# A product's two weight halves in one transfer instead of two, in a fused attention and gated-FFN layer

## The chip, the cores and the metric

The kernel runs on one core of one Trainium2 chip, as one launch. The time is that of the device in microseconds (us), from the first instruction to the last; lower is better. Before the change it is 2654.52 us, the median of three runs (2654.34 to 2654.75).

## The reference, cut to what matters

```python
x = L0_attn_x                                   # (4, 512, 1024) fp32
xn = _layernorm(x)                              # (x - mean) / sqrt(var + 1e-5)
# attention: 32 query heads, 8 key/value heads, head dimension 128
q, k, v = heads(xn @ Wq.T), heads(xn @ Wk.T), heads(xn @ Wv.T)
q, k = _rmsnorm(q, q_norm_w), _rmsnorm(k, k_norm_w)
scores = einsum('bkgqd,bksd->bkgqs', group(q), k) / sqrt(128)
attn = softmax(scores + causal_alibi_bias)
s = einsum('bkgqs,bksd->bkgqd', attn, v).reshape(b, 512, 4096) @ Wo.T
# gate: a linear layer with 8 low-rank adapters merged into it
g = silu(xn @ W.T + bias + sum_n lora(xn, A[n], B[n]))
return x + s * g
```

## The kernel before, in words

The work is cut into 32 groups n = 8 b + g: b is one of the four sequences, g one of the eight key/value heads. A group is the key head, the value head, four query heads and 128 columns of the gate. Each group has four steps (n, j), one for each query head. Inside a step every engine runs its own list, written out by hand in program order: TensorE (PE) computes scores and the attention product of the head before, turns rows, computes products of the *next* group's projection, then the output projection of an earlier head, then turns this head's probabilities (`step` at L697).

**The projection.** The columns of a group (896 of them, as two halves of 448) are computed by a seven-product scheme over 2 x 2 blocks. The products are called P1, P2, P6, P7, P4, P5, P3 in the order in which they are computed. Group n+1 has P1 and P2 in step (n, 0), P6 and P7 in (n, 1), P4 in (n, 2), P5 and P3 in (n, 3). A product runs for two row tiles t = 0, 1 (`piece`, L538). Its weights are two halves h = 0, 1, each 128 partitions x 896 fp32 values, 448 KB. Every fp32 product is made of three matmuls on a high and a low part of each operand (`three`, L507), so a piece is 12 matmuls: six on half 0, then six on half 1. `w_half` is incremented after half 0 of t = 1, `u_done` after half 1.

**The weights' way.** Halves are numbered w = 14 n + 2 p + h, and half w uses place w % 4 of the buffers `wh` and `wl`. So the two halves of a product lie side by side in places 0, 1 or 2, 3, and a product's places come free when the product two before it is done. SyncE (SP) loads the half from the scratch tensor `wu` in DRAM into `wl` (L302, `load_w`); ScalarE (ACT) copies it into `wh`, rounded (`split_w`, L785 to L788); GpSimd (POOL) subtracts and leaves the low part in `wl` (`low_w`, L1081); then PE may use it (`w_ready`). SP waits for `w_half` before it loads half 0 and for `u_done` before half 1; ACT waits for the half's own semaphore, one of four `w_in`. ACT is told to split P6 and P7 at the end of step (n, 0), P4 and P5 at the end of (n, 1), P3 at the end of (n, 2), P1 and P2 at the end of (n, 3): the first of each pair stands between the first three turned probability tiles and the fourth (`probs_hi`, L858), the second after the fourth. P3 stands there by itself.

**Where the scratch comes from.** In the first sequence the block sums of the weights are still being made. For groups up to 7 SP loads raw weights (`load_weights`, L327), stores three tiles as they are (L347, L348), POOL makes four sums (`weight_sums`, L1132 to L1137), SP stores those (L355), and loads of `wu` wait for these stores (`prep_bst`, `prep_tst`, L299 and L301). All of these are issued by SP in one written order (`step` at L428), so each instruction waits for those ahead of it.

**VectorE (DVE)** works in order as well. At the end of step (n, 2) it makes the low part of the fourth turned tile (L1284), adds the last output bank (L1344), takes two score maxima of the next step (L1319), scales the key rows and the first query rows of group n+1 (L1274), then takes the last two maxima. PE turns those rows (L588) in step (n, 3) before it computes P5.

For the very first P3 the load is issued by ACT (`load_first`, L804 to L812), one half ahead of each of two groups of squares.

Of the kernel before, what the change touches and what calls it, by code (L numbers as in the profile page):

```python
# [7 lines left out]
F32 = mybir.dt.float32  # L8
# [4 lines left out]
H, HKV, HD = 32, 8, 128  # L13
# [9 lines left out]
NG = BATCH * HKV  # L23
# [9 lines left out]
NP = 7  # L33
HW = 2 * NP
P1, P2, P6, P7, P4, P5, P3 = range(NP)
# [8 lines left out]
KEPT = [P1, P2, P3, P5, P7, P4, P6]  # L44
# [25 lines left out]
def loads_into_slot(w):  # L70

    return (w - DIRECT) // 4 + (-1 if w >= LATER else 1)
# [43 lines left out]
def u_count(n, p, t):  # L116
    return HW * n + 2 * p + t + 1
# [10 lines left out]
def build_layer(nc, x_tok, x_first, xT, wa, wo, wT, lora_a, lora_bt, lw, ffn_b, qw, kw, rel, slopes,  # L128
                ident, outT):
    with ExitStack() as ctx:  # L130
        def sb(name, shape, dt=F32):
            return ctx.enter_context(nc.sbuf_tensor(name, shape, dt))
# [4 lines left out]
        def sem(name):  # L137
            return ctx.enter_context(nc.semaphore(name))
# [3 lines left out]
        wu = nc.dram_tensor("wu", [HKV * HW, P, 2 * HALF], F32).ap()  # L142
# [6 lines left out]
        wh, wl = sb("wh", [P, 4, 2, HALF], F32R), sb("wl", [P, 4, 2, HALF], F32R)  # L149
# [38 lines left out]
        weff_out = [sem("weff_out0"), sem("weff_out1")]  # L188
        prep_in, prep_bst = [sem("prep_in0"), sem("prep_in1")], [sem("prep_bst0"), sem("prep_bst1")]
        prep_tst = [sem("prep_tst0"), sem("prep_tst1")]  # L190
        w_in = [sem(f"w_in{i}") for i in range(4)]
        b_in = [sem("b_in0"), sem("b_in1")]
        gate_out = sem("gate_out")
        fin_in = [sem(f"fin_in{i}") for i in range(4)]
# [3 lines left out]
        u_done, w_half = sem("u_done"), sem("w_half")  # L198
# [46 lines left out]
        def prep_tile(g, h, a, c):  # L245

            at = 2 * a + c
            return prep_place(g, h)[:, at * 896:at * 896 + 896].rearrange("p (k n) -> p k n", k=2)
# [21 lines left out]
        def w_slot(t, w, f32=False):  # L270
            ap = t[:, w % 4].rearrange("p k n -> p (k n)")
            return ap.bitcast(F32) if f32 else ap

        def need(eng, semaphore, value):
            if value > 0:
                eng.wait_ge(semaphore, value)
# [6 lines left out]

        @block.sync
        def _(sp):
            def load_w(w):
                if w >= HW * NG:
                    return
                n, at = divmod(w, HW)
                p, h = divmod(at, 2)  # L290
                if w >= 4:
                    n_old, at_old = divmod(w - 4, HW)
                    if h == 0:
                        sp.wait_ge(w_half, NP * n_old + at_old // 2 + 1)
                    else:
                        sp.wait_ge(u_done, u_count(n_old, at_old // 2, 1))
                if n < HKV:
                    if p in (P1, P2, P3):
                        sp.wait_ge(prep_bst[h], 32 * (n + 1))  # L299
                    else:  # L300
                        sp.wait_ge(prep_tst[h], 16 * (n + 1))  # L301
                sp.dma_start(w_slot(wl, w, True), wu[(n % HKV * 2 + h) * NP + KEPT.index(p)]  # L302
                             ).then_inc(w_in[w % 4], 16)

            def load_product(n, p):
                for h in range(2):
                    load_w(HW * n + 2 * p + h)

            def load_b(v):
                if not 0 <= v < NV:  # L310
                    return
                need(sp, out_done, 4 * v - 4)
                if v < 32:
                    sp.wait_ge(wo_copied, 16 * (v + 1))
                sp.dma_start(wb_lo[:, v % 2, :].bitcast(F32), wo_in[v % 32]).then_inc(b_in[v % 2], 16)

            def copy_b(v):
                if v < 32:
                    need(sp, wo_copied, 16 * v)
                    sp.dma_start(wo_in[v], wo[v]).then_inc(wo_copied, 16)  # L320
# [52 lines left out]
            def load_result(b, half):  # L373
                if half == 0 and b + 1 < BATCH:
                    sp.wait_ge(tr_done, TR["x", b + 1, 2 * NP - 1] + 1)
                sp.wait_ge(gate_out, 16 * (HKV * b + 4 * half + 4))
                for c in range(4 * half, 4 * half + 4):
                    x, gate = result_slots(b, c)
                    if b + 1 < BATCH or half == 0:
                        need(sp, res_out[c % 4], 16 * (2 * b + half))  # L380
                    landed = fin_last if b + 1 == BATCH and half == 1 else fin_in
                    sp.dma_start(x, xT[b * NK + c]).then_inc(landed[c % 4], 16)
                    sp.dma_start(gate, gate_dram[b % 2 * NK + c]).then_inc(landed[c % 4], 16)
# [44 lines left out]
            def step(n, j):  # L428
# [23 lines left out]
                if j == 1:  # L452
                    if n == 0:
                        load_product(1, P4)
                    if new is not None:
                        store_halves(new, 0)
                    if n > 0:
                        load_product(n + 1, P4)
                    if g == 0 and ending is not None:
                        store_result(ending, 0)  # L460
                    load_product(n + 1, P5)
# [44 lines left out]
        def _(pe):  # L506
# [59 lines left out]
            def turn_x(key):  # L566
                _, b, f = key
                p = FILLS[f // 2]
                row, col = FILL_AT[p]
                if p in FILL_SUM:  # L570
                    pe.wait_ge(sum_ready, 4 * b + FILL_SUM[p])
                else:
                    if b == 0 and p != P4:
                        pe.wait_ge(x_scaled, 2)
                    else:
                        pe.wait_ge(ln_ready, scaled_rows(b, 4 if p == P4 else 2))
                bank = turn_bank(key)
                for i in range(2):
                    for t in range(2):
                        c = col + (2 * (f % 2) + i) * P  # L580
                        mm = pe.transpose(bank[:, i * 256 + t * P:i * 256 + t * P + P],  # L581
                                          xtok[:, row + t, c:c + P], ident_sb[:])
                mm.then_inc(tr_done, 1)
# [172 lines left out]
        def _(act):  # L756
            act.preload_act_table_set("natural_log_exp_and_others")

            def split_first(p):

                a, c = QUARTER[p]
                for h in range(2):
                    w = 2 * p + h
                    if p in (P1, P2):
                        act.wait_ge(prep_in[h], 128)
                        act.wait_ge(gate_cols, NK)
                    else:
                        act.wait_ge(prep_t[h], 4 if p in (P4, P5) else 3)
                        if h == 0:
                            act.wait_ge(w_half, p - 1)  # L770
                        else:
                            act.wait_ge(u_done, u_count(0, p - 2, 1))
                    act.activation(wh[:, w % 4], prep_tile(0, h, a, c), ACT.Copy).then_inc(w_hi_done, 1)
# [10 lines left out]
            def split_w(w):  # L784
                if w >= HW * NG:  # L785
                    return
                act.wait_ge(w_in[w % 4], 16 * loads_into_slot(w))
                act.activation(w_slot(wh, w), w_slot(wl, w, True), ACT.Copy).then_inc(w_hi_done, 1)  # L788

            def split_later(p, h):  # L790
# [10 lines left out]
                    act.wait_ge(u_done, u_count(0, at // 2, 1))  # L801
                act.activation(wh[:, w % 4], prep_tile(1, h, *QUARTER[p]), ACT.Copy).then_inc(w_hi_done, 1)

            def load_first(h):  # L804

                w = 2 * P3 + h
                if h == 0:
                    act.wait_ge(w_half, P4 + 1)
                else:
                    act.wait_ge(u_done, u_count(0, P4, 1))  # L810
                act.wait_ge(prep_bst[h], 32)
                act.dma_start(w_slot(wl, w, True), wu[h * NP + KEPT.index(P3)]).then_inc(w_in[w % 4], 16)  # L812

            def split_product(n, p):
                for h in range(2):
                    split_w(HW * n + 2 * p + h)
# [21 lines left out]
            def square_rows(n, p, t):  # L838

                if p == P2:  # L840
                    act.wait_ge(u_act, u_act_count(n, P2, t))
                else:
                    act.wait_ge(u_dve, u_dve_count(n, p, t))
                squares(("q0", "q1", "k") if p in (P2, P4) else ("q2", "q3"),
                        t if p in (P2, P3) else t + 2,
                        8 * n + 2 * (P2, P4, P5, P3).index(p) + t)
# [112 lines left out]
            act.wait_ge(fb_in, 16)  # L959
            split_first(P4)  # L960
            split_first(P5)
            for h in range(2):
                load_first(h)
                square_rows(0, P4, h)
            rsqrt(0, 0)
            split_product(0, P3)
# [686 lines left out]
```

## Time and profile before

| what | value |
|---|---|
| median of three runs | 2654.52 us |
| profiled execution, whole | 2655.72 us |
| profiled execution, span | 2653.9 us |
| PE matmul busy | 2583.1 us, 97% |
| PE weight load busy | 2288.9 us, 86% |
| POOL busy | 1718.0 us, 65% |
| ACT busy | 1764.6 us, 66% |
| DVE busy | 1699.8 us, 64% |
| mean granted TensorE clock | 0.995 of full speed |

The profile is one execution. Busy time is time in which an engine has an instruction in work; matmuls overlap one another, so a busy PE is not one without any loss. The page also gives the chain of waits (followed back from the last instruction), the waits of each engine with the instruction that ended them, and for DMA the time from issue to landing. The four waits of interest are: SP for PE (the places come free), ACT for a transfer, POOL for ACT, and PE for POOL or DVE. Line numbers are those of the kernel before.

### The profile page before, as it was taken

To read this page: it belongs to the slowest core of one execution; us is meant where nothing else is said; L and a number is where in the kernel's file an instruction comes from. 1 tells how busy PE (TensorE), PEld (TensorE's weight loads), DVE (VectorE), ACT (ScalarE), POOL (GpSimd) and SP (SyncE) were. 2 spreads that over 40 slices of the span, in tenths; PEclk is the share of its full clock that TensorE was granted. 3 is DMA by queue.
4 is the path that set the end of the run, shared out by engine and by line. 5 is a ranking of instruction groups with operands and counts; after the bars stand their busy time and mean duration, and the time that the engine had idled before them with its cause. 6 is when DMAs were issued, how large, how long until landed. Compare 5 with 4: busy or idle time off the path is not lost.

```text
span 2653.9 us, 39893 instructions
## 1 busy us (share of the span) xinstructions
PE 2583.1 (97%) x13840; PEld 2288.9 (86%) x13840; DVE 1699.8 (64%) x3533; ACT 1764.6 (66%) x4633; POOL 1718.0 (65%) x839
## 2 busy tenths in 40 slices
PE   6789999999999999999999999999999999999997
PEld 5778888888888888888888888888888888888886
DVE  7565656666766665666667666666666756656656
ACT  4565666767767666667766667666777666667764
POOL 3577887785767565655667756565666766656555
PEclk9899999999999999999999999999999999999999
DMA  7868878875354333433344433433334533333323
GB/s 283 289 219 278 265 261 272 271 258 166 118 171 154 113 106 118 140 112 118 106 137 155 128 119 111 144 106 118 109 104 137 189 106 108 115 116 112 112 78 131
DMA packets 171896, 414.78 MB, mean 156 GB/s; under 512 B 31024, under 2 KB 63920, under 8 KB 170800
## 3 DMA queue, kind: packets, MB, share of 16 engines
q1 hardware_dynamic: 170144, 410.19, 47.1%
q8 instruction: 112, 1.84, 0.3%
q10 hardware_dynamic: 1552, 2.04, 0.2%
q14 instruction: 88, 0.72, 0.1%
HBM read 339.81 MB, written 89.13 MB: 162 GB/s over the span
## 4 chain that ended last, share of the span: by engine, by line
PE 90%; DVE 3%; DMA 2%; POOL 2%; ACT 1%; SPq 1%; issue 0%; ACTq 0%; POOLq 0%; DVEq 0%
PE proj L508 21%; PE proj L510 21%; PE proj L509 21%; PE tr L608 5%; PE tr L588 3%; PE sc L508 3%; PE sc L509 3%; PE sc L510 3%; PE ot L509 3%; PE ot L510 3%; PE ot L508 3%; DMA wu<-xtok 1%; PE tr L581 1%; DMA wl<-wu 1%; POOL wl L1081 1%
## 5 line engine op out<-in xcount | busy, mean ns | idle before, releaser
L1081 POOL TENSOR_TENSOR wl<-wl,wh 128x896 fp32r<-128x896 f32 x428 | 909.1, 2156 | 552.3 <-ACT wh L788 552.2
L508 PE MATMUL proj<-wh,xh 128*128 128x448 f32 x1792 | 670.7, 374 | 7.3 <-ACT raw L827 2.2
L509 PE MATMUL proj<-wl,xh 128*128 128x448 f32 x1792 | 657.9, 367 | 0.0
L510 PE MATMUL proj<-wh,xl 128*128 128x448 f32 x1792 | 657.8, 367 | 0.0
L1092 POOL TENSOR_TENSOR wb_lo<-wb_lo,wb_hi 128x1024 fp32r<-128x1024 f32 x128 | 307.7, 2404 | 303.7 <-ACT wb_hi L822 303.7
L879 ACT ACTIVATE misc<-misc,negmax 128x128 f32<-128x128 f32 (+3 forms) x512 | 286.7, 565 | 266.3 <-DVE negmax L1319 266.1
L508 PE MATMUL proj<-o_hi,wb_hi 128*128 128x512 f32 x1024 | 425.2, 415 | 7.4 <-DVE acc L1344 3.5
L1344 DVE TENSOR_TENSOR acc<-acc,proj 128x512 f32<-128x512 f32 x476 | 324.8, 683 | 149.7 <-PE proj L510 147.8
L858 ACT ACTIVATE pT_hi<-tr 128x512 fp32r<-128x512 f32 (+3 forms) x512 | 197.5, 440 | 325.9 <-PE tr L608 325.9
L510 PE MATMUL proj<-o_hi,wb_lo 128*128 128x512 f32 x1024 | 403.6, 394 | 0.0
L509 PE MATMUL proj<-o_lo,wb_hi 128*128 128x512 f32 x1024 | 401.3, 392 | 0.0
L788 ACT ACTIVATE wh<-wl 128x896 fp32r<-128x896 f32 x428 | 387.9, 965 | 19.7 <-DMA wl<-wu 19.2
L1314 DVE TENSOR_TENSOR raw<-raw,proj 128x448 f32<-128x448 f32 x320 | 197.4, 617 | 301.9 <-PE proj L510 300.1
L508 PEld LDWEIGHTS proj<-wh,xh 128*128 128x128 f32 x1792 | 337.9, 189 | 37.1 <-ACT raw L827 4.9
L510 PEld LDWEIGHTS proj<-wh,xl 128*128 128x128 f32 x1792 | 337.4, 188 | 30.0
L509 PEld LDWEIGHTS proj<-wl,xh 128*128 128x128 f32 x1792 | 338.1, 189 | 27.8
L1319 DVE CUSTOM_DVE_ANT_0 misc<-sc,misc 128x128 f32<-128x128 f32 (+3 forms) x512 | 240.9, 487 | 175.9 <-PE sc L510 174.7
L1284 DVE TENSOR_TENSOR pT_lo<-tr,pT_hi 128x512 fp32r<-128x512 f32 (+3 forms) x512 | 226.6, 484 | 74.7 <-ACT pT_hi L858 74.4
L834 ACT ACTIVATE junk<-raw 128x128 f32<-128x128 f32 x640 | 189.8, 301 | 97.2 <-DVE raw L1314 93.4
L886 ACT ACTIVATE misc<-misc,rs_inv 128x128 f32<-128x128 f32 (+3 forms) x512 | 245.2, 558 | 1.0 <-DVE rs_inv L1325 1.0
L508 PEld LDWEIGHTS proj<-o_hi,wb_hi 128*128 128x128 f32 x1024 | 193.4, 189 | 51.7 <-DVE acc L1344 4.1
L1100 POOL TENSOR_SCALAR misc<-misc,slope 128x512 f32<-128x512 f32 x128 | 233.6, 1825 | 4.1 <-DMA misc<-rel 4.1
(135 smaller groups left out, 4438.1 us busy)
## 6 DMA issues: line engine op xcount, KB each, us to landing
wl<-wu SPq DMA_DIRECT2D x426, 448.0 KB, 3.9
wb_lo<-wo_in SPq DMA_DIRECT2D x128, 512.0 KB, 3.3
wu<-xtok SPq DMA_DIRECT2D x13, 1792.0 KB, 9.7
wo_in<-wo SPq DMA_DIRECT2D x32, 512.0 KB, 6.2
xtok<-wa SPq DMA_DIRECT2D x52, 256.0 KB, 4.0
wu<-xtok SPq DMA_DIRECT2D x13, 896.0 KB, 6.2
gate_dram<-misc SPq DMA_DIRECT2D x32, 256.0 KB, 5.0
xtok<-xT SPq DMA_DIRECT2D x28, 256.0 KB, 5.1
```

The lines of the kernel that those rows point to most:

```text
L508: pe.matmul(out, hi_l, hi_r, start=first, stop=False, skip_group_check=onto)
L509: pe.matmul(out, hi_l, lo_r, start=False, stop=False, skip_group_check=onto)
L510: return pe.matmul(out, lo_l, hi_r, start=False, stop=last, skip_group_check=onto)
L788: act.activation(w_slot(wh, w), w_slot(wl, w, True), ACT.Copy).then_inc(w_hi_done, 1)
L879: act.activation(p, p, ACT.Exp, bias=negmax[:, i:i + 1], scale=-1.0, accum_out=rowsum[:, i:i + 1]).then_inc(exp_done, 1)
L886: ins = act.activation(p, p, ACT.Copy, scale=rs_inv[:, i:i + 1])
L1081: pool.tensor_tensor(w_slot(wl, w), w_slot(wl, w, True), w_slot(wh, w), ALU.subtract).then_inc(w_ready, 1)
L1092: pool.tensor_tensor(wb_lo[:, v % 2, :], wb_lo[:, v % 2, :].bitcast(F32), wb_hi[:, v % 2, :], ALU.subtract).then_inc(wb_ready, 1)
L1100: pool.tensor_scalar(bias_sb[:, m % 2, :], rel_sb[:], slope[:, m % H:m % H + 1], None, ALU.mult).then_inc(bias_ready, 1)
L1284: dve.tensor_tensor(dst, bank, hi, ALU.subtract).then_inc(tr_free, 1)
L1319: dve.tensor_tensor_reduce(prob[:, P_AT[i]:P_AT[i] + w], sc_ps[i % 2][:, 0:w], bias_sb[:, m % 2, S - w:S], -1.0, 3e38, ALU.add, ALU.min, n ...
L1344: dve.tensor_tensor(a, a, bank, ALU.add).then_inc(out_free, 1)
```

## The change

A product's two halves are loaded by one `dma_start` of 896 KB, which writes both neighbouring places and reads the two rows of `wu` that lie NP = 7 rows apart. SP waits for `u_done` alone (no longer for `w_half`), and for both halves' stores where the load is of the first sequence. There are two `w_in` semaphores instead of four; ACT's wait for each half is a wait for the whole product's transfer. `load_first` issues one transfer ahead of both groups of squares. What is split, subtracted and multiplied, and in which order, stays as it was.

```diff
-        w_in = [sem(f"w_in{i}") for i in range(4)]
+        w_in = [sem("w_in0"), sem("w_in1")]
+        def w_places(w):
+            return wl[:, w % 4:w % 4 + 2].rearrange("p s k n -> p s (k n)").bitcast(F32)
+        def w_rows(n, p):
+            at = n % HKV * HW + KEPT.index(p)
+            return wu[at:at + NP + 1:NP].rearrange("s p n -> p s n")
...
-            def load_w(w):
-                if w >= HW * NG:
+            def load_product(n, p):
+                if n >= NG:
                     return
-                n, at = divmod(w, HW)
-                p, h = divmod(at, 2)
+                w = HW * n + 2 * p
                 if w >= 4:
                     n_old, at_old = divmod(w - 4, HW)
-                    if h == 0:
-                        sp.wait_ge(w_half, NP * n_old + at_old // 2 + 1)
-                    else:
-                        sp.wait_ge(u_done, u_count(n_old, at_old // 2, 1))
+                    sp.wait_ge(u_done, u_count(n_old, at_old // 2, 1))
                 if n < HKV:
-                    if p in (P1, P2, P3):
-                        sp.wait_ge(prep_bst[h], 32 * (n + 1))
-                    else:
-                        sp.wait_ge(prep_tst[h], 16 * (n + 1))
-                sp.dma_start(w_slot(wl, w, True), wu[(n % HKV * 2 + h) * NP + KEPT.index(p)]
-                             ).then_inc(w_in[w % 4], 16)
-            def load_product(n, p):
-                for h in range(2):
-                    load_w(HW * n + 2 * p + h)
+                    for h in range(2):
+                        if p in (P1, P2, P3):
+                            sp.wait_ge(prep_bst[h], 32 * (n + 1))
+                        else:
+                            sp.wait_ge(prep_tst[h], 16 * (n + 1))
+                sp.dma_start(w_places(w), w_rows(n, p)).then_inc(w_in[w // 2 % 2], 16)
...
-                act.wait_ge(w_in[w % 4], 16 * loads_into_slot(w))
+                act.wait_ge(w_in[w // 2 % 2], 16 * loads_into_slot(w))
...
-            def load_first(h):
-                w = 2 * P3 + h
-                if h == 0:
-                    act.wait_ge(w_half, P4 + 1)
-                else:
-                    act.wait_ge(u_done, u_count(0, P4, 1))
-                act.wait_ge(prep_bst[h], 32)
-                act.dma_start(w_slot(wl, w, True), wu[h * NP + KEPT.index(P3)]).then_inc(w_in[w % 4], 16)
+            def load_first():
+                act.wait_ge(u_done, u_count(0, P4, 1))
+                for h in range(2):
+                    act.wait_ge(prep_bst[h], 32)
+                act.dma_start(w_places(2 * P3), w_rows(0, P3)).then_inc(w_in[P3 % 2], 16)
...
+            load_first()
             for h in range(2):
-                load_first(h)
                 square_rows(0, P4, h)
```

## Rows read from the trace of the kernel before

**Rows 1.** Engines' busy time in three stretches: us, busy (x instructions), PEclk, DMA share, GB/s
```profile
110.00:235.00 125.00, 108.36 (x551) 94.60 (x552) 73.04 (x143) 73.50 (x185) 91.73 (x44) 0.95 0.74 255
235.00:620.00 385.00, 384.21 (x2059) 341.39 (x2058) 246.07 (x509) 258.82 (x691) 307.91 (x149) 1.00 0.79 263
620.00:2560.00 1940.00, 1936.06 (x10476) 1724.55 (x10476) 1242.47 (x2646) 1334.94 (x3514) 1227.87 (x597) 1.00 0.39 124
```
**Rows 2.** Who waited for line 1274: us in total, times
```profile
  PEld tr L588: 5.5, 28
```
**Rows 3.** ACT's waits for the halves (us, times, longest), 110 to 235, then 620 to 2560
```profile
ACT wh L788 <- DMA wl<-wu: 13.6, 8, 3.8
ACT wh L788 <- DMA wl<-wu: 4.1, 4, 1.4
```
**Rows 4.** SP's loads of one P3, then the second alone: start, us, what
```profile
1036.31 1.53 SPq L302 DMA_DIRECT2D wl<-wu  x2
1037.52 0.32 SPq L302 DMA_DIRECT2D wl<-wu  x1
```
**Rows 5.** Issue to landing, us (last): half 0, half 1, then a `wb` load
```profile
wl<-wu SPq DMA_DIRECT2D x1, 448.0 KB, 3.3
wl<-wu SPq DMA_DIRECT2D x1, 448.0 KB, 3.9
wb_lo<-wo_in SPq DMA_DIRECT2D x1, 512.0 KB, 3.2
```
**Rows 6.** ACT in time order around the splits of that P3
```profile
1041.84 1.80 ACT L788 ACTIVATE wh<-wl 128x896 fp32r<-128x896 f32 x2
1043.52 0.29 ACT L858 ACTIVATE pT_hi<-tr 128x128 fp32r<-128x128 f32 x1
```
**Rows 7.** DVE in time order just after
```profile
1043.84 0.29 DVE L1284 TENSOR_TENSOR pT_lo<-tr,pT_hi 128x128 fp32r<-128x128 f32 x1 [0.35 <-ACT pT_hi L858]
...
1044.76 0.28 DVE L1319 CUSTOM_DVE_ANT_0 misc<-sc,misc 128x128 f32<-128x128 f32 x1
...
1045.34 2.91 DVE L1274 SCALAR_TENSOR_TENSOR raw<-raw,tmp 128x512 f32<-128x512 f32 x2
```
**Rows 8.** PE's weight loads of the turned query rows there
```profile
1048.30 0.42 PEld L588 LDWEIGHTS tr<-ident_sb,raw 128*128 128x128 f32 x4 [0.18 <-DVE raw L1274]
```
**Rows 9.** ACT behind queued loads, then the POOL work that follows
```profile
177.79 0.96 ACT L788 ACTIVATE wh<-wl 128x896 fp32r<-128x896 f32 x1 [1.37 <-DMA wl<-wu]
179.65 0.95 ACT L788 ACTIVATE wh<-wl 128x896 fp32r<-128x896 f32 x1 [0.74 <-DMA wl<-wu]
181.69 0.95 ACT L788 ACTIVATE wh<-wl 128x896 fp32r<-128x896 f32 x1 [1.09 <-DMA wl<-wu]
...
178.83 6.26 POOL L1081 TENSOR_TENSOR wl<-wl,wh 128x896 fp32r<-128x896 f32 x3 [0.20 <-ACT wh L788]
```
**Rows 10.** Engines and DMA from 60 to 75, columns as in Rows 1
```profile
60.00:75.00 15.00, 15.00 (x75) 13.61 (x74) 6.01 (x10) 5.36 (x17) 8.43 (x4) 1.00 1.00 381
```
**Rows 11.** Second halves of P3, issue to landing: n = 1, 5 and 7
```profile
wl<-wu SPq DMA_DIRECT2D x1, 448.0 KB, 5.5
wl<-wu SPq DMA_DIRECT2D x1, 448.0 KB, 4.6
wl<-wu SPq DMA_DIRECT2D x1, 448.0 KB, 4.2
```
**Rows 12.** P5 by contrast: its second load, and ACT's splits of it
```profile
1022.24 0.32 SPq L302 DMA_DIRECT2D wl<-wu  x1
1028.42 1.81 ACT L788 ACTIVATE wh<-wl 128x896 fp32r<-128x896 f32 x2
```
**Rows 13.** Chain of waits in the opening, in time order: start, us, what
```profile
129.60 8.29 DMA wl<-wu
...
174.40 3.37 DMA wl<-wu
...
194.12 6.84 DMA wu<-xtok
```

## The prediction

> **What bounds the kernel now.** I read three things in this order: busy time by stretch, the waits, then the time order around one load.
>
> By stretch, PE is the bound almost everywhere. From 620 to 2560 us it is busy for 1936 of 1940 us, and from 235 to 620 for 384.2 of 385; only from 110 to 235 does it idle for 16.6 of 125, at a granted clock of 0.95 and with the DMA engines 74% busy [rows 1]. So outside the opening an edit is worth what it does to PE, and nothing in the load path waits for long: from 620 to 2560 ACT waits for a weight half 4 times, 4.1 us in all, while in the opening it does so 8 times for 13.6 us [rows 3].
>
> That PE is busy doesn't mean that it has slack towards the others. Its loads of the turned query rows end an idle moment behind DVE's scaling (line 1274) 28 times in the run, 5.5 us in all [rows 2], once in nearly each of the 31 groups that have a next one. These waits are tiny, but they say that in step (n, 3) DVE is exactly on time: what comes later on DVE there comes later on PE. So I followed that place backwards. PE's load at 1048.30 waits 0.18 us for DVE [rows 8]; DVE has been working without a break since its low part of the fourth turned tile at 1043.84, and that one sat 0.35 us for ACT's high part [rows 7]; ACT made it at 1043.52, right behind the two splits of P3 that began at 1041.84 [rows 6]. The chain from P3's split to PE has no gap in it. The reader is to see that the load of P3 is the one load whose lateness PE would feel.
>
> **The change part by part.**
>
> *When the transfer starts.* SP waits for the same `u_done` as half 1 did. For the P3 shown, half 0 was issued at 1036.31 and half 1 at 1037.52 [rows 4]; the joint one goes out at 1037.52, so half 0 starts 1.21 us later and half 1 not earlier. Nothing else is queued behind a new wait: SP stood there for half 1 already. One issue of 0.32 us goes for each product [rows 4]; SP spends its time waiting for PE there, which hides it, and in the opening it is worth a few times 0.3 us.
>
> *How long it takes.* No load of 896 KB stands in this trace. One of 448 KB that has the queues to itself lands 3.3 us after its issue, one of 512 KB after 3.2 [rows 5]. The half behind another lands 3.9 us after its own issue: at 1041.42, where the first landed at 1039.61, 1.8 us later [rows 4, 5]. In the opening, where several are queued and ACT waits for each, its splits start at 177.79, 179.65 and 181.69, 1.86 and 2.04 us apart [rows 9]. So a queued 448 KB costs 1.8 to 2.0 us, and the joint transfer lands after 3.3 + 1.85 = 5.15 us. Bounds: from 60 to 75 us the engines moved 381 GB/s [rows 10], at which the second 459 kB take 1.2 us, 4.5 in all; a difference of 2.0 and a tenth or two for a longer issue make 5.5. I take 5.15, by the nearest rows, which are the same transfers.
>
> The Trainium skill, "DMA: Bandwidth & Descriptors", section "Anatomy of one DMA", gives a fixed cost of about 2.0 us for each transfer plus its bytes at 436 GB/s (fitted for another way of issuing). By that 448 KB take 3.05 us, close to the 3.3 here, and 896 KB take an estimated 4.1 us, which would be in time. The trace speaks against the rate: at it the second half would find the engines free and land after 3.05 us too, not after 3.9 [rows 5].
>
> *P3 in the steady part.* Before, half 0 was there at 1039.61 and half 1 at 1041.42, and ACT came at 1041.84: no wait, with 0.4 us left. Now ACT needs the whole transfer for its first split: 1037.52 + 5.15 = 1042.67, a wait of 0.83 us. The margin is 1041.84 - 1037.52 = 4.32 us. By the chain above the 0.83 us goes to the fourth tile's high part, DVE's low part, its score maxima and scaling, and PE. It isn't won back, since PE is the bound and each group's P4 shifts with it. This occurs in 24 groups, n = 7 to 30 (in n = 6 two layer-norm scalings stand before the split): 24 x 0.83 = 19.9 us. By the bounds of 4.5 and 5.5 us it is 24 x 0.18 = 4.3 and 24 x 1.18 = 28.3.
>
> *P3 in groups 1 to 5.* A store of 1792 KB is in flight, and half 1 landed 5.5 us after its issue in n = 1 and 4.6 in n = 5 [rows 11], against 4.2 in n = 7 and 3.9 in n = 11. Waits of 5.7 to 6.6 less 4.32 us would follow if the joint transfer added 1.1 as above; but the store has drained further when half 0 starts later. I take 1.4 us each, 7 us in all, between 2 and 11.
>
> *The other products.* P5's second half was issued at 1022.24 and its first split is at 1028.42 [rows 12]: a margin of 6.2 us against 5.15. P1, P2, P4, P6 and P7 have that or more in the steady part, so their cost is nothing while a transfer takes less than 6.2 us. Three P5 loads (one at each new sequence, issued behind result stores) already end waits of 1.2 to 1.4 us; 1.7 us more there is partly absorbed, 1 us each at most, within the range.
>
> *The opening.* There the chain of waits runs through these loads [rows 13]. P5 of group 1, issued at 129.60, lands after 8.3 us; the joint one ends with its half 1, some 1.2 us later. Then P1 and P2 of group 2: half 1 of P1 could only go at 174.40, when the store for it had landed, and half 0 was already there. Now half 0 waits as well: four halves queue from 174.40, P1 lands at 179.65 rather than 177.79, P2 at about 183.6 rather than 181.69. POOL, which did the last three low parts by 185.09 [rows 9], has four after 180.6, until 189: 3.9 us later, and its sums and the store at 194.12 [rows 13] follow. P6 and P7 of group 2, behind that store, repeat the pattern. I count 1.2 + 3.9 and about 2, less 2 of gaps on the way: 5 us, between 1 and 9. The very first P3, issued by ACT, is costed at nothing: PE idles behind block sums later in that stretch; without that cover it would be 1 to 2 us.
>
> *Sum.* 19.9 + 7 + 5 = 31.9 us on the profiled execution's 2655.72 (span 2653.9), which stands 1.2 us above the median of 2654.52. So the forecast is 2654.5 + 31.9, about 2686 us.
>
> **The rivals.**
>
> *The joint transfer is in time* (4.3 us or less). For it: the skill's fit, and the 381 GB/s stretch comes near. Against: three differences of 1.8 to 2.0 us. P3 costs nothing, only the opening does: 2654.5 + 2.5 = 2657, within 0.2%.
>
> *ACT waits but PE doesn't.* It needs slack between ACT and PE of 0.8 us; the trace shows 0.35 us of idle in the wrong direction (DVE waiting for ACT). Opening and early groups alone, about 2661.
>
> *Faster.* In the opening ACT's waits are ended by half 1. If one transfer with one completion makes a queued 448 KB cheaper than 1.9 us (four transfers become two), these halves land earlier than now and the chain of loads, splits, sums and stores shortens. It decides where 896 KB land sooner than half 1 does now, 3.9 us after the issue. It can give back at most the 13.6 us of waits there [rows 3]; perhaps 5 us, 2649. Against: the bytes are the same and the engines 74% busy.
>
> *More of the same.* If transfers take over 6.2 us where others are in flight, P5, P2 and P7 turn late too: another 15 us, about 2702.
>
> **How the numbers follow.** The forecast has 0.64, in time 0.12, absorbed 0.06, faster 0.08, more of the same 0.10. A measurement here can tell about 0.2%, 5.3 us. Slower by more than that: 0.64 + 0.06 + 0.10 = 0.80; within: 0.12; faster: 0.08. The forecast's own range is 2664 (bounds of 4.3, 2 and 3) to 2702 (28.3, 11 and 8). Down to 2657 it takes in the two cases of little loss: 2657 to 2702.
>
> **What would show it.** Right: ACT's line 788 waits for `wl` in nearly every group just before P3's split, 0.5 to 1.2 us each, some 25 us in all after 235 us; PE's waits for line 1274, or for the score maxima just before, grow to the same sum; SP issues one load where it issued two, landing 5.0 to 5.3 us later in the steady part. Wrong: landings under 4.4 us; ACT's waits present and PE's stretch from 620 to 2560 no longer than before; or the opening shorter.

## The result, and the profile after

The changed kernel takes 2686.09 us, the median of four runs (2683.0 to 2687.38), against 2654.64 us for the kernel before beside it: a ratio of 1.0115, 95% interval 1.0098 to 1.0133. It is slower by 31.5 us. The profiled execution has a span of 2684.9 us against 2653.9, so the two traces differ by 31.0 us.

Where the 31.0 us lie can be read from one instruction that SP issues in the same place in both kernels, its `wb` load in step (n, 0). In the changed kernel, for n = 2, 7 and 31 (start, us, what):

```profile
272.76 0.33 SPq L316 DMA_DIRECT2D wb_lo<-wo_in  x1
...
680.72 0.33 SPq L316 DMA_DIRECT2D wb_lo<-wo_in  x1
...
2608.83 0.32 SPq L316 DMA_DIRECT2D wb_lo<-wo_in  x1
```

Before, the same three stood at 266.60, 665.91 and 2577.92. So 6.2 us are lost in the opening, 8.7 more up to group 7, and 16.1 from there to group 31. The same subtraction, made for each experiment below, gives this table of differences from the kernel before, in us of the profiled executions. Each row is one execution: kernels in which nothing or little is joint behind the opening stand between -0.7 and +1.2 in the last column, and that is about how finely it can be read.

| kernel | opening, to (2, 0) | from there to (7, 0) | from there to (31, 0) |
|---|---|---|---|
| changed kernel | +6.2 | +8.7 | +16.1 |
| P3 in two, others joint | +8.0 | 0.0 | +1.2 |
| only P3 joint | -0.2 | +6.5 | +14.3 |
| all in two, both late | -0.7 | -0.2 | +0.6 |
| the same, half 1 first | +2.9 | +4.4 | +7.2 |
| joint from group 8 | -1.2 | +0.2 | +14.9 |
| joint, P3's split moved back | +7.8 | +3.8 | +24.6 |
| two, P3's split moved back | -1.5 | +5.2 | +22.0 |
| joint in group 2 alone | +5.3 | 0.0 | -0.7 |
| joint, near rows from group 8 | +9.2 | +10.5 | +8.8 |
| two, half 0 of P3 split early | 0.0 | +4.1 | +14.8 |
| cut by partitions | +15.2 | +17.8 | +81.1 |
| cut by columns | +6.8 | +4.6 | +17.8 |

The chain of waits over one P3 of the changed kernel, in order of time (start, us, what), shows the path of the loss:

```profile
1055.25 4.87 DMA wl<-wu
1060.14 1.79 ACT wh L789 x2
1061.93 0.17 ACT pT_hi L856
1062.13 0.07 DVE pT_lo L1282
1062.34 0.24 DVE acc L1342
1062.93 0.28 DVE misc L1317
1063.22 0.34 DVE misc L1317
1063.57 2.37 DVE raw L1272
1065.98 1.26 PE tr L589 x8
```

It starts at the joint load and ends at PE. The load's own row among the DMA issues (last number: us from issue to landing):

```profile
wl<-wu SPq DMA_DIRECT2D x1, 896.0 KB, 4.9
```

Of the same P3, the three waits that it makes, in the timeline (start, busy us, what; in brackets the wait and what ended it): ACT before its split of P3, PE's loads before the third score tile, and PE before the key and query rows, which already waited a little before [rows 2, 8].

```profile
1060.14 1.79 ACT L789 ACTIVATE wh<-wl 128x896 fp32r<-128x896 f32 x2 [0.45 <-DMA wl<-wu]
...
1063.28 0.19 PEld L509 LDWEIGHTS sc<-kT_hi,qT_hi 128*128 128x128 f32 x1 [0.50 <-DVE negmax L1317]
...
1065.98 0.42 PEld L589 LDWEIGHTS tr<-ident_sb,raw 128*128 128x128 f32 x4 [0.20 <-DVE raw L1272]
```

Of ACT's waits for `wl`, from 110 to 241, 241 to 640 and 640 to 2590 us of the changed kernel (us, times, longest):

```profile
ACT wh L789 <- DMA wl<-wu: 17.0, 7, 6.6
ACT wh L789 <- DMA wl<-wu: 9.7, 7, 2.8
ACT wh L789 <- DMA wl<-wu: 21.9, 27, 2.9
```

The last of these was 4 times, 4.1 us [rows 3]; it is now 27 times, once for P3 in each of the 24 groups that were named (13.9 us in all) and once for P5 at each of the three new sequences. PE's weight loads behind the score maxima and behind the scaling, first in the changed kernel in that stretch, then in the kernel before from 640 to 2560 us:

```profile
PEld sc L509 <- DVE negmax L1317: 16.0, 25, 1.8
PEld tr L589 <- DVE raw L1272: 8.4, 45, 0.2
```

```profile
PEld tr L588 <- DVE raw L1274: 4.0, 22, 0.2
...
PEld sc L508 <- DVE negmax L1319: 2.5, 3, 1.8
```

So 13.5 of the 17.9 us that are new stand at the maxima, which DVE takes behind the fourth tile. Two of the 24 groups, 13 and 21, lose nothing (their length differs from before by 0.03 us), although ACT waits 0.3 us for P3 there: in both kernels PE has just waited about 0.65 us for a turned tile, and no wait at the maxima follows.

In the opening PE now has this stretch (columns as in [rows 1]):

```profile
110.00:241.00 131.00, 112.39 (x548) 99.59 (x549) 72.56 (x142) 71.55 (x180) 91.92 (x44) 0.88 0.67 233
```

The mean granted clock there is 0.88 of full speed; before, it was 0.95 in the same stretch, with PE busy for 114.4 us. How much of the opening's loss is the clock's was not separated.

### The profile page after: what moved, and what is told of

Same layout as the page of the kernel before. It is cut to its first block, busy times and chain, and to the rows that moved or that the text cites. A ratio compares the mean times of both kernels' runs of the same rounds, so it can differ in the third digit from the quotient of the medians.

```text
span 2684.9 us, 39633 instructions
## 1 busy us (share of the span) xinstructions
PE 2600.0 (97%) x13840; PEld 2293.8 (85%) x13840; DVE 1697.7 (63%) x3533; ACT 1765.9 (66%) x4633; POOL 1716.6 (64%) x839
## 3 DMA queue, kind: packets, MB, share of 16 engines
q10 hardware_dynamic: 1536, 2.04, 0.2%
## 4 chain that ended last, share of the span: by engine, by line
PE 80%; DMA 7%; DVE 5%; ACT 4%; POOL 3%; issue 1%; SPq 0%; ACTq 0%; POOLq 0%; DVEq 0%
PE proj L511 19%; PE proj L509 19%; PE proj L510 19%; DMA wl<-wu 5%; PE tr L609 4%; PE tr L589 3%; PE sc L509 3%; PE sc L510 3%; PE sc L511 3%; PE ot L510 2%; PE ot L511 2%; PE ot L509 2%; ACT wh L789 2%; DVE raw L1272 1%; DMA wu<-xtok 1%
```

## The experiments

All were timed in five rounds beside the kernel before, whose median was then 2655.0 to 2655.7 us. To choose by product, the kernels got one predicate, `joint(n, p)`, true for all products in the changed kernel; where it is false, the two transfers of the kernel before are issued, with a semaphore for each place. The edits are shown shortened, and "in two" means that `joint` is false for every product.

**P3 apart.**

```diff
-    return True
+    return p != P3
```

> P3's halves alone go back to two transfers with their own waits; the five or six other products of each group stay joint. Theory A (ACT's first split of P3 waits for a joint transfer that lands 4.9 to 5.2 us after its issue, where its margin is 4.3 us, and the wait runs through DVE to PE): all that the change cost behind the opening goes, 15.3 us in groups 7 to 30 and about 8 in groups 1 to 5, and the opening's 8 us stay: 2662 to 2665 us. Rival B (transfers of 896 KB are worse as such, by what they do to each other and to the stores in all places): most of the cost stays, 2678 to 2686. Rival C (the loss is all in the opening, the later shift follows from it): 2680 to 2686.

Measured: 2662.13 us (2660.22 to 2664.89), ratio 1.0027 (1.0016 to 1.0038). The loss behind the opening is gone, 0.0 and +1.2 us in the table, and 8.0 us in the opening stay. Six joint products of seven cost next to nothing once PE is the bound.

**Only P3 joint.**

```diff
-    return True
+    return p == P3 and n > 0
```

> The complement: only P3 of groups 1 to 31 is joint, all others are two transfers. Theory A: the opening is as before, P3 costs 15.3 us in groups 7 to 30 and some 8 in groups 1 to 5: 2676 to 2680 us, with ACT waiting 0.3 to 0.8 us for wl before P3's split in each of these groups. Rivals B and C: 2655 to 2662.

Measured: 2676.36 us (2675.59 to 2679.38), ratio 1.0084 (1.0070 to 1.0098): nothing in the opening, 6.5 and 14.3 us behind it. The two complements, 6.4 and 20.6 us on their medians, add up to 27.0 of the 31.5; in their profiled executions, 9.2 and 20.6 to 29.8 of 31.0. The rivals that put the loss on all transfers or on the opening alone are out.

**The later issue without the joint completion.** In two, and:

```diff
-                if h == 0:
-                    sp.wait_ge(w_half, NP * n_old + at_old // 2 + 1)
-                else:
-                    sp.wait_ge(u_done, u_count(n_old, at_old // 2, 1))
+                sp.wait_ge(u_done, u_count(n_old, at_old // 2, 1))
```

> Two transfers of 448 KB for every product, but both are issued after u_done, half 0 first: the later issue of the change without the joint completion. Theory A: half 0 of P3 lands 3.3 us after its issue, 1.0 us before ACT comes, and half 1 about 5.1 us after, about when its own split is due (5.2 us): no loss in the steady part, in the opening 0 to 4 us: 2654 to 2659 us. Rival D (what costs is that the load starts 1.2 us later, whatever it is cut into): 2675 to 2686.

Measured: 2655.44 us (2653.58 to 2657.63), ratio 1.0000 (0.9991 to 1.0009). Starting half 0 later by 1.2 us costs nothing. For one P3, SP's two issues and ACT's split in the timeline, and then the landing of each transfer (us, last):

```profile
1036.69 0.80 SPq L319 DMA_DIRECT2D wl<-wu  x2
1037.05 0.43 SPq L319 DMA_DIRECT2D wl<-wu  x1
...
1041.01 1.81 ACT L816 ACTIVATE wh<-wl 128x896 fp32r<-128x896 f32 x2
```

```profile
wl<-wu SPq DMA_DIRECT2D x1, 448.0 KB, 3.5
wl<-wu SPq DMA_DIRECT2D x1, 448.0 KB, 4.2
```

Half 0 is there at 1036.69 + 3.5 = 1040.2, 0.8 us before ACT, and half 1 at 1037.05 + 4.2 = 1041.25, when ACT still has half 0 in work. Two things follow. What costs behind the opening is that ACT's *first* split has to wait for the *last* byte. And the second half came 4.56 us after the first one's issue (median of the 24 groups 4.5), 1.1 us after the first half (median 1.1), so a 448 KB transfer that is queued right behind another costs 1.1 us, not 1.85. (The figure of 4.2 to 4.3 us "after the first's issue" in two expectations is this 4.2 counted from the wrong issue.)

**Half 1 ahead of half 0.** The last kernel, and:

```diff
-                    for h in range(2):
+                    for h in (1, 0):
                         load_half(w + h, n, p, h)
```

> As the kernel with two transfers that are both issued after u_done, but half 1 is issued first and half 0 behind it. Nothing is joint; half 0, which ACT splits first, lands where the joint transfer would. Theory A: 5.0 to 5.2 us from issue to half 0, a wait of 0.6 to 0.9 us before P3's split and the full cost behind the opening (15 to 22 us in groups 7 to 30, 6 to 9 in groups 1 to 5), with an opening about as in the joint kernel: 2680 to 2692 us. Rival B (being joint is what costs): as the one with half 0 first, 2654 to 2660.

Measured: 2672.02 us (2667.03 to 2673.05), ratio 1.0061 (1.0048 to 1.0073), 16.3 us slower. The same two transfers as in the kernel that lost nothing, only in the other order: nothing is joint, and what ACT needs first comes last. That is the mechanism without the change's form. The size was forecast too large (25 to 37 us), because half 0 lands about 4.5 us after the first issue, just at the margin, and not 5.1: ACT waits 0.2 to 0.7 us for P3 in 10 of the 24 groups and not at all in the others. A loss of 7.2 us in the steady part instead of 16.1 fits a landing earlier by 0.4 us.

**Joint from group 8 on.**

```diff
-    return True
+    return n >= HKV
```

> Joint transfers only from group 8 on, two before. Theory A: the steady part's loss stands by itself, without the opening and groups 1 to 7: 23 groups of about 0.6 us, 13 to 15 us in all, 2668 to 2671 us. Rival C (the later shift is a consequence of the opening, or of the clock lost there): 2655 to 2658.

Measured: 2669.94 us (2668.51 to 2670.48), ratio 1.0057 (1.0044 to 1.0069). The steady loss stands by itself, 14.9 us, and the opening has no part in it. (The expectation counts 23 groups; `n >= HKV` makes P3 of groups 8 to 31 joint, which are the same 24 loads as in the changed kernel.)

**P3's split moved behind the fourth turned tile, joint and in two.** ACT in step (n, 2):

```diff
-                split_product(n + 1, P3)
                 probs_hi(m, 3)
+                split_product(n + 1, P3)
```

> All products joint as in the changed kernel, but ACT splits P3 behind the fourth turned tile instead of ahead of it. Theory A (the wait reaches PE because the fourth tile's high part is queued on ACT behind P3's split): ACT's wait for P3 all but goes and what is left of it reaches nothing on PE; only the opening's 6 to 8 us stay: 2658 to 2664 us. Rival F (PE loses through POOL's late low parts of P3, or through the transfer's load on memory): 2678 to 2686.

> Two transfers as in the kernel before, with P3's split behind the fourth turned tile. Theory A: DVE's 0.35 us of waiting for that tile goes, and with it PE's 0.18 us behind DVE in 22 to 28 groups: 3 to 6 us faster than before, 2650 to 2653 us. Rival G (the 0.18 us are hidden on PE anyway): 2655 to 2656.

Measured: 2692.43 us joint (ratio 1.0139, 1.0125 to 1.0153) and 2681.69 us in two (1.0102, 1.0088 to 1.0116). Both were forecast wrong, and they are the runs that taught most. One part of the forecast held: with the split moved, ACT no longer waits for P3 in the steady part (its 3 waits there are for P5), and the joint load adds 2.7 us to that part (24.6 against 22.0) in place of 16.1. But with the kernel's own transfers the move alone costs 26.7 us. The fourth tile does come earlier; the scaling of keys and queries does not. POOL and DVE of the kernel in two, moved:

```profile
1051.19 4.64 POOL L1119 TENSOR_TENSOR wl<-wl,wh 128x896 fp32r<-128x896 f32 x2 [3.64 <-ACT wh L816]
...
1052.58 3.80 DVE L1312 SCALAR_TENSOR_TENSOR raw<-raw,tmp 128x512 f32<-128x512 f32 x2
```

The two scalings take 3.80 us; in the kernel before, 2.91 [rows 7]; where POOL has nothing in work, one takes 0.68 and two of them 1.29. They end 0.55 us after POOL's low parts end, 1056.38 against 1055.83. In the kernel before, POOL's low parts of P3 ran from 1042.88 to 1047.09 and the pair ended at 1048.25, 1.16 us after; in the changed one from 1061.17 to 1065.38 and at 1066.53, 1.15 us after:

```profile
1042.88 4.21 POOL L1081 TENSOR_TENSOR wl<-wl,wh 128x896 fp32r<-128x896 f32 x2 [2.55 <-ACT wh L788]
```

```profile
1061.17 4.21 POOL L1079 TENSOR_TENSOR wl<-wl,wh 128x896 fp32r<-128x896 f32 x2 [3.15 <-ACT wh L789]
...
1063.49 3.04 DVE L1272 SCALAR_TENSOR_TENSOR raw<-raw,tmp 128x512 f32<-128x512 f32 x2
```

So DVE is held while POOL subtracts, and the later POOL stands relative to DVE, the longer. Not every DVE instruction is: the low part of the fourth tile, which has one of its inputs in PSUM, took 0.29 us beside the same subtraction [rows 7]. The Trainium skill, "SBUF — State Buffer", section "Who interferes with whom", says that a VectorE instruction with two SBUF inputs contends with a GpSimd instruction that reads SBUF, for ports that are an exclusive lock; the traces agree, with these durations. 24 groups times the 0.89 us by which the pair grew in this one are 21.4 us, of the table's 22.0.

PE's weight loads behind the scaling in that kernel, 640 to 2550 us, where before they were 0.2 us at most:

```profile
PEld tr L616 <- DVE raw L1312: 27.5, 24, 2.0
```

**Half 0 of P3 split early, in two.** Half 0 is split ahead of the first three turned tiles, half 1 where P3 was. ACT in step (n, 2):

```diff
+                split_w(HW * (n + 1) + 2 * P3)
                 for k in range(3):
                     probs_hi(m, k)
-                split_product(n + 1, P3)
+                split_w(HW * (n + 1) + 2 * P3 + 1)
                 probs_hi(m, 3)
```

> Two transfers as before, and ACT splits half 0 of P3 ahead of the first three turned tiles, in its 0.96 us of waiting for PE, half 1 where it was. Theory M (DVE's scaling of keys and queries is held by POOL's low parts of P3, which is why the pair takes 2.9 us beside them and 1.3 without): POOL ends about 2 us earlier, the pair takes 1.3 to 1.6 us, PE's 0.18 us of waiting goes in each group: 2648 to 2652 us. Rival N (the pair's length has another cause): pair still 2.9 us, 2654 to 2656; if the early split holds up the turned tiles on ACT, 2656 to 2665.

Measured: 2674.60 us (2669.92 to 2677.26), ratio 1.0070 (1.0058 to 1.0083), where a gain was forecast, and slower than the rival's range too. The theory on DVE and POOL holds: the scaling pair of P3's groups takes 1.3 to 1.8 us, mostly 1.5, in place of 2.9, and the mean of all 160 scalings falls from 998 to 749 ns. Yet a group's period stays, 78.82 us against 78.84, so PE's 0.18 us behind DVE had been worth nothing. Of the 14.8 us lost in the steady part, 12.9 stand in two groups, 13 and 21, the ones with the next sequence's layer-norm factors, where POOL's subtraction now meets five tiny DVE instructions (start, us); the other 1.9, and the 4.1 us in groups 2 to 6, were not followed up:

```profile
1202.86 4.27 POOL L1123 TENSOR_TENSOR wl<-wl,wh 128x896 fp32r<-128x896 f32 x2 [0.54 <-ACT wh L816]
...
1202.99 2.01 DVE L1267 TENSOR_TENSOR tmp_x<-tmp_x,var_x 128x4 f32<-128x4 f32 x1
1205.24 1.91 DVE L1271 TENSOR_TENSOR rinv_x<-rinv_x,tmp_x 128x4 f32<-128x4 f32 x1
```

The wait of PE's weight loads that follows, in the table of waits (us, times, longest):

```profile
PEld tr L636 <- DVE pT_lo L1326: 4.7, 1, 4.7
```

The two shown take 0.16 us each in the kernel before. Each is held for the rest of a subtraction, and PE's next weight load waits 4.7 us.

**Joint in group 2 alone.**

```diff
-    return True
+    return n == 2 and p in (P1, P2, P6, P7)
```

> Only the four products P1, P2, P6 and P7 of group 2 are joint: those of the opening whose second half has to wait for a store of its own while the first may go at once. Theory A (these two places cost the opening its 6 to 8 us; P5 of group 1 adds 1): 2659 to 2662 us. Rival J (the opening's loss is spread over all its loads, or is absorbed later): 2655 to 2657.

Measured: 2658.50 us (2657.41 to 2661.85), ratio 1.0015 (1.0006 to 1.0024): 3.2 us on the median, 5.3 us in the opening of its profiled execution, which is 1.8 us above the median. So 4 of SP's 213 transfers hold the greater part of the opening's loss.

**Near rows.**

```diff
-            return wu[at:at + NP + 1:NP].rearrange("s p n -> p s n")
+            far = NP if n < HKV else 1
+            return wu[at:at + far + 1:far].rearrange("s p n -> p s n")
```

> As the changed kernel, but from group 8 on the joint transfer reads two neighbouring rows of wu in place of two that lie seven rows (3.2 MB) apart; so from there the second half of each product has the wrong weights, everything else is done as before. Theory K (the distance of the two reads makes the joint transfer 0.6 us slower than two transfers together): landings of 4.3 us and no steady loss, about 2670 us. Rival L (one transfer of 256 packets costs that by itself): 4.9 to 5.0 us and 2682 to 2688 us.

From group 8 on this kernel leaves out each product's own second half and loads the row next to the first in its place, so it shows times alone. Measured: 2676.85 us (2675.25 to 2684.28), ratio 1.0084 (1.0070 to 1.0098); the profiled execution is the slowest of the five, 7.4 us above the median. A joint load of P3 now lands 4.7 us after its issue in place of 4.9 (medians of the 24 groups 4.6 and 5.0), and the steady loss is 8.8 us in place of 16.1. Its landing, and ACT's wait for it:

```profile
wl<-wu SPq DMA_DIRECT2D x1, 896.0 KB, 4.7
```

```profile
1063.32 1.79 ACT L817 ACTIVATE wh<-wl 128x896 fp32r<-128x896 f32 x2 [0.27 <-DMA wl<-wu]
```

Neither theory as stated: the distance of the two rows makes about 0.3 of the 0.4 us between the joint load (median 5.0) and two transfers issued together (4.5). How it does so wasn't tried. The run shows how steep the place is: 0.3 us a load are 7 us on the kernel.

**Cut by partitions, and by columns.**

```diff
-                sp.dma_start(w_places(w), w_rows(n, p)).then_inc(w_in[...], 16)
+                for rows in (slice(0, P // 2), slice(P // 2, P)):
+                    sp.dma_start(w_places(w)[rows], w_rows(n, p)[rows]).then_inc(w_in[...], 16)
```

The second kernel cuts `[:, :, cols]` instead, into columns 0 to 447 and 448 to 895.

> Each product's weights in two transfers again, issued back to back after u_done, but cut by partitions: each brings 64 partitions of both halves, and ACT waits for both. The completion is as joint as in the change, only the number of transfers differs. In the kernel with both late the second of two such transfers was there 4.2 to 4.3 us after the first's issue, the joint one needs 4.9 to 5.0. Theory H (one transfer of 256 packets is slower by itself than two of 128): landing of the second 4.2 to 4.4 us after the first's issue, little wait at P3 (margin 4.3 to 4.4), steady part 0 to 4 us, opening 6 to 8: 2661 to 2667 us. Rival I (the size and the rows read decide, however they are cut): 4.9 to 5.0 us, 2682 to 2688.

> Each product's weights in two transfers issued back to back after u_done, each with all 128 partitions and the first or second 448 columns of both halves; ACT waits for both. Jointly complete as in the change, in two transfers, but with rows of 1792 bytes instead of 3584. Theory H (one transfer of 896 KB is slower than two of 448 KB): second landing 4.2 to 4.5 us after the first's issue, steady loss under 5 us, opening 6 to 8: 2660 to 2668 us. Rival O (pieces of half the size cost more than the second transfer saves): 4.9 us or more, 2682 us and up.

Measured: 2769.65 us by partitions (ratio 1.0427, 1.0412 to 1.0441) and 2683.68 us by columns (1.0111, 1.0097 to 1.0125). Theory H, that one transfer is slower than two merely for being one, forecast 4.2 to 4.5 us and is not borne out. The columns kernel alone doesn't refute it, since its pieces of 1792 bytes may cost what the second transfer saves, and both its transfers still read the two far rows; but with the near rows one transfer is within 0.1 to 0.2 us of two. Landing of the second transfer of a P3 (us, last), by partitions in the first fence and by columns in the second:

```profile
wl<-wu SPq DMA_DIRECT2D x1, 448.0 KB, 6.2
```

```profile
wl<-wu SPq DMA_DIRECT2D x1, 448.0 KB, 4.5
```

By columns it was issued 0.40 us behind the first, so all is there after 4.9 us, as with one joint transfer, and the time is near the joint kernel's. By partitions it is 0.62 + 6.2 = 6.8 us, and even the first of the two took 4.9 for its 448 KB, where a half over 128 partitions takes 3.3 [rows 5], or 3.5 with another right behind it, as above. The Trainium skill, "SBUF — State Buffer", section "Door 1: The DMA port swizzle (why `[64,N]` ≈ `[32,N]`)", says that partitions 0 to 63 reach only 8 of the 16 ports, and 64 to 127 the other 8; a slower transfer of the same bytes is what this run shows.

## Why the prediction was right, point by point

**The place: right.** P3 was named as the one load whose lateness PE would feel, in 24 groups and groups 1 to 5. Undoing P3 alone takes nearly all of that away, doing P3 alone brings nearly all of it. Not all the places lose: groups 13 and 21 lose nothing.

**The chain: right in its ends, incomplete in the middle.** ACT, the fourth turned tile, DVE's maxima, the scaling, PE: the chain of waits of the changed kernel shows these, and most of PE's new waits stand at the maxima. That DVE is "exactly on time" was not worth what it seemed: with half 0 split early DVE is earlier, and PE gains nothing. And "DVE has been working without a break" was a misreading. A row of 2.91 us for two scalings that take 1.29 alone is a wait inside an instruction. DVE hangs on ACT by two ways, through the tile and through POOL's subtraction of P3, and the joint load delays both alike. The moved split cuts only the first way and makes the second later, and so it cost more than it recovered.

**The trigger: half right.** The forecast put the cost on ACT waiting for the whole transfer, and allotted nothing to the wait for `u_done` beyond the 1.2 us. The run with both transfers late shows the later issue to be free as long as half 0 comes by itself, and the reversed pair shows that the order of arrival is enough. With a joint load the 1.2 us do count: issued with half 0 at 1036.31 it would by estimate have been there at 1041.2, before ACT came. No run tried that, since half 1's place isn't free then.

**The landing time: nearly the right number, by luck.** 5.15 us was forecast; over the 24 groups the median is 4.96, from 4.6 to 5.3 and once 6.2. It was built as 3.3 plus 1.85 for a queued half. Two transfers issued together are there after 4.5 us, so a queued half costs 1.1 us; the 1.8 us of [rows 4, 5] holds the 1.21 us between the two issues. The spacings of 1.86 and 2.04 us [rows 9] don't repeat: the same two are 1.24 and 1.72 us in the kernel with both late, and P2's whole 896 KB land 2.40 us behind P1's in the changed one; why they vary there wasn't tried. Some 0.4 us more came with the joint form, most of it with the distance of the rows. The two errors offset each other. The fit in the Trainium skill, "DMA: Bandwidth & Descriptors", section "Anatomy of one DMA", by which the estimate was 4.1 us (fitted for another way of issuing), was 0.8 to 0.9 us too low, and with it went the rival that the load would be in time.

**The sizes.** For each group 0.83 us was forecast; in the changed kernel ACT waits 0.2 to 0.8 for P3 and once 1.7, 0.58 on average, the P3 shown 0.45, and PE loses 16.1 / 24 = 0.67 on average (three of these groups also have the P5 load behind result stores, where ACT waits up to 2.9 us). So 19.9 us were forecast and 16.1 measured. Groups 1 to 5: 7 against 8.7, which is for groups 2 to 6, as group 1's P3 falls into the opening. The opening: 5 against 6.2. The sum, 31.9 against 31.0, is closer than its terms: the steady term was too large by 3.8, the two others too small by 2.9. (The range took 3 and 8 us for the opening where the text has 1 and 9; by the latter it would be 2662 to 2703, and nothing changes.)

**The opening: right in the place.** P1 and P2 of group 2 were forecast to end POOL's four low parts by 189, 3.9 us later than the 185.09 before; they end at 189.53:

```profile
181.28 8.25 POOL L1079 TENSOR_TENSOR wl<-wl,wh 128x896 fp32r<-128x896 f32 x4 [7.64 <-ACT wh L789]
```

Half 0 could go before the store for half 1 had landed, and now waits for it. Between executions this term moves: 6.2 us in the changed kernel, 9.2 us in the near-rows kernel, whose groups up to 7 are the same, and 8.0 us with P3 apart.

**The rivals.** The faster one had its deciding point at 3.9 us for 896 KB; behind 700 us no joint load of the changed kernel landed under 4.39.

**What stays open.** Why reading two rows 3.2 MB apart in one transfer costs about 0.3 us more than neighbouring ones, why single landings take 5.2 us and more, and what the lower clock in the opening is worth.

None of the versions beats the kernel before; the two-transfer kernel with both issues late equals it.

## What to carry to other kernels

A transfer that feeds two consumers in order should be cut where the consumers are: joining the parts makes the first consumer wait for the last byte, and in the opening for the later of two stores. That cost 31 us here, and no run shows a gain from the issue that it saves. Before joining or moving anything, measure for each load how long before its first use the last byte lands (in the kernel before 0.4 us for the P3 shown and 0.2 in the median, against a median of 1.5 us or more for each of the others), and follow the consumer's queue to the bound engine. And read the duration of an instruction against its twin elsewhere: where the same instruction took over twice as long in one place, it was waiting there, and the order of another engine was part of its schedule.

## What the runs showed of the hardware that wasn't expected

- DVE instructions with two inputs in SBUF are held by a POOL subtraction until it ends: two scalings take 1.29 us alone and 2.9 to 3.8 beside it, and a 128x4 product went from 0.16 to 2.01 us. The profile shows this as a long instruction and not as idle time before it.
- Two 448 KB loads issued 0.36 us apart are complete 4.5 us after the first issue, one of 896 KB from two rows 3.2 MB apart after 5.0, from neighbouring rows after 4.6 (medians of the P3 loads of 24 groups).
- A 448 KB load into 64 partitions takes 4.9 us, into 128 partitions 3.3 to 3.5.
